# Attention over image pixels: steps of two key tiles for 256 queries, and sums in two of four banks

## The reference

```python
xf = x.reshape(b, c, n)                                   # 8, 128, 1024
q = einsum('oc,bcn->bon', Wq, xf) + bq[None, :, None]     # 64 x 1024
k = einsum('oc,bcn->bon', Wk, xf) + bk[None, :, None]
v = einsum('oc,bcn->bon', Wv, xf) + bv[None, :, None]     # 128 x 1024
attn = softmax(einsum('bci,bcj->bij', q, k), axis=-1)     # 1024 x 1024
out = einsum('bcn,bmn->bcm', v, attn)
return gamma * out + x
```

## Time and profile before

| | |
|---|---|
| median of 3 runs | 234.23 us (234.16 to 234.97) |
| the profiled execution | 234.46 us, its span 232.6 us |
| granted clock of PE in it | 0.996 of full speed |
| PE busy | 221.2 us, 95% |
| DVE, ACT, POOL busy | 175.9, 179.3, 200.4 us (76%, 77%, 86%) |
| DMA moved | 24.39 MB, mean 105 GB/s |

### The profile page before, as it was taken

How to read it: one execution, slowest core, us unless ns; L and a number is a source line. 1 busy time by engine, 2 the same in 40 slices (tenths; PEclk the granted TensorE clock), 3 DMA queues, 4 the chain that set the end, 5 groups by cost and what they waited for, 6 DMA issues and landing times.

```text
span 232.6 us, 4731 instructions
## 1 busy us (share of the span) xinstructions
PE 221.2 (95%) x1608; PEld 189.2 (81%) x1608; DVE 175.9 (76%) x289; ACT 179.3 (77%) x345; POOL 200.4 (86%) x174
## 2 busy tenths in 40 slices
PE   6997999999999999999999999999999999999981
PEld 5464988888788878889789988898798899899880
DVE  1687388796888877796978968797878969696374
ACT  2768887788688877789787886789777878788942
POOL 8688998589996899789996899968996998879990
PEclk9999999999999999999999999999999999999998
DMA  3637900670709325490527607192215803011002
GB/s 85 204 151 175 272 7 2 138 184 3 224 14 232 75 70 159 99 219 3 168 60 175 143 0 230 34 231 55 98 41 120 195 4 135 2 48 45 0 3 90
DMA packets 18023, 24.39 MB, mean 105 GB/s; under 512 B 9936, under 2 KB 10832, under 8 KB 18000
## 3 DMA queue, kind: packets, MB, share of 16 engines
q1 hardware_dynamic: 17552, 23.89, 39.6%
q10 hardware_dynamic: 448, 0.20, 0.3%
HBM read 8.59 MB, written 4.19 MB: 55 GB/s over the span
## 4 chain that ended last, share of the span: by engine, by line
POOL 56%; issue 24%; PE 11%; DVE 4%; ACT 1%; DMA 1%; POOLq 1%; ACTq 0%
POOL weight_lo L458 38%; POOL x_turned_sb L466 7%; POOL total L472 6%; POOL values_b L450 3%; POOL x_lo L439 3%; DVE neg_max L822 2%; PE sums L597 2%; PE work L541 2%; DMA w_qk<-in_L_conv_Wk 1%; PE scores L578 1%; PE scores L579 1%; PE scores L535 1%; PE sums L613 1%; PE scores L639 1%; PE sums L524 1%
## 5 line engine op out<-in xcount | busy, mean ns | idle before, releaser
L458 POOL TENSOR_TENSOR weight_lo<-weight,weight_hi 128x512 bf16<-128x512 f32 x90 | 122.9, 1387 | 21.0 <-ACT weight_hi L756 20.9
L822 DVE TENSOR_REDUCE neg_max<-work 128x1 f32<-128x512 f32 x120 | 80.8, 684 | 26.5 <-PE work L541 26.4
L753 ACT ACTIVATE weight<-scores 128x512 f32<-128x512 f32 x128 | 76.9, 601 | 19.4 <-PE scores L579 14.2
L597 PEld LDWEIGHTS sums<-values,weight_hi 128*128 128x128 f32 x504 | 77.2, 188 | 10.6 <-issue 0.5
L597 PE MATMUL sums<-values,weight_hi 128*128 128x258 f32 x504 | 80.6, 282 | 0.1
L756 ACT ACTIVATE weight_hi<-scores 128x512 fp32r<-128x512 f32 x128 | 77.0, 601 | 0.0
L578 PE MATMUL scores<-q_hihi,k_hilo 128*128 128x512 f32 x128 | 53.4, 417 | 0.7 <-ACT weight_hi L756 0.7
L541 PE MATMUL work<-k_hilo,q_hihi 128*128 128x512 f32 x120 | 48.6, 409 | 2.0 <-DVE neg_max L822 1.6
L579 PE MATMUL scores<-q_lomax,k_hione 128*128 128x512 f32 x128 | 50.4, 394 | 0.0
L853 DVE TENSOR_TENSOR weight_lo<-weight,weight_hi 128x512 bf16<-128x512 f32 x38 | 39.1, 1028 | 4.5 <-ACT weight_hi L756 4.5
L613 PE MATMUL sums<-values_b,weight_lo 128*128 128x130 bf16 x496 | 34.3, 221 | 0.0
(11 more groups left out here) (80 smaller groups left out, 162.3 us busy)
## 6 DMA issues: line engine op xcount, KB each, us to landing
x_turned_sb<-in_x_turned SPq DMA_DIRECT2D x8, 512.0 KB, 5.3
out<-y_sb SPq DMA_DIRECT2D x15, 256.0 KB, 2.5
x_sb<-in_x SPq DMA_DIRECT2D x7, 512.0 KB, 4.7
q_hihi<-qk_hi SPq DMA_DIRECT2D x12, 256.0 KB, 4.2
q_lomax<-qk_lo SPq DMA_DIRECT2D x7, 256.0 KB, 5.0
k_hione<-qk_hi SPq DMA_DIRECT2D x7, 256.0 KB, 5.0
k_hilo<-qk_hi SPq DMA_DIRECT2D x6, 256.0 KB, 3.1
k_hilo<-qk_lo SPq DMA_DIRECT2D x6, 256.0 KB, 5.0
```

The costliest lines, as they stand in the source:

```text
L458: pool.tensor_tensor(weight_lo[:, r], weight[:, r], weight_hi[:, r], ALU.subtract).then_inc(weight_lo_pool_done, 1)
L597: last = pe.matmul(sums[:, it, 0:VCOLS], weight_hi[:, r, tile(it)], values[p][:, j], start=(j == 0), stop=False)
L753: act.activation(weight[:, r], scores[:, s % 2], ACT.Exp)
L822: dve.reduce_max(neg_max[:, t, h:h + 1], place, AX.X, negate=True).then_inc(neg_max_done, 1)
```

## The change

- A step has two key tiles and 256 queries. Its scores are four matmuls of 256 columns, its sums four matmuls of 258 columns: two key tiles by two query tiles. ACT's instructions keep their size.
- A part is four steps: 256 queries against all 1024 keys. Its two query tiles take two of the four banks of `sums`, and the next part takes the other two. A low burst ends each part.
- At a part's end ACT copies the first half of the sums of both tiles, DVE inverts two denominators and adds the copy to the sums in place, in PSUM, and one loop later it makes y of each tile from PSUM with one instruction (multiply by the inverse, add `x_turned_sb`). `total` and POOL's `scale` are gone.
- PE waits for y of the part before last ahead of a part's first sums, in place of `sums_freed`.
- The second v projection moves from step 1 of its own image to step 13 of the image before, POOL's bias additions from steps 7 and 14 to steps 11 and 15 of the image before, x's remainders from 4 and 6 to 3 and 7; `DVE_LOW` loses one of five steps.
- The last part has two tiles; DVE does all of it: inverse, first half times inverse plus x, second half times inverse plus that. Its stores are one on SP and one on ACT.
- In the ramp the first scores need the maxima of two query tiles only; the other two follow as a second rounding, transposition (`mt` at step 0) and row. q of image 0's second half, the second v projection and image 1's q/k projections come behind the first scores, the remainder of that v is DVE's. `load_x_turned(0)` is issued ahead of `spread_by_halves`. The early maxima are shared out anew.

```diff
+PAIR = 2
+PART = PAIR * TILE
+PARTS = CHUNKS * CHUNK_TILES // PAIR
+PART_STEPS = ALL_STEPS // PARTS
...
-DVE_LOW = (0, 4, 8, 13, 15)
+DVE_LOW = (0, 4, 8, 12)
...
-EARLY_MAXES = {5: (2, 0, 1), 6: (2, 1, 2), 7: (2, 3, 2), 8: (2, 5, 1), 9: (2, 6, 1), 10: (2, 7, 1),
-               11: (3, 0, 2), 12: (3, 2, 1), 13: (3, 3, 1), 14: (3, 4, 1), 15: (3, 5, 1), 16: (3, 6, 1), 17: (3, 7, 1)}
+EARLY_MAXES = {0: (1, 1, 2), 1: (1, 3, 2), 2: (1, 5, 2), 3: (1, 7, 1),
+               6: (2, 0, 1), 7: (2, 1, 2), 8: (2, 3, 1), 9: (2, 4, 1), 10: (2, 5, 1), 11: (2, 6, 2),
+               12: (3, 0, 1), 13: (3, 1, 1), 14: (3, 2, 1), 15: (3, 3, 2), 16: (3, 5, 1), 17: (3, 6, 2)}
...
-    if k == 1 and b > 0:
-        jobs.append(("v", b, 1))
+    if b == 0 and k == 0:
+        jobs.append(("mt", 0, 1))
     if b == 0 and k == 4:
         jobs.append(("mt", 1, 0))
     if k in (8, 12) and b + 2 < BATCHES:
         jobs.append(("qk", b + 2, (8, 12).index(k)))
-    if k == 9 and b + 1 < BATCHES:
-        jobs.append(("v", b + 1, 0))
+    if k in (9, 13) and b + 1 < BATCHES:
+        jobs.append(("v", b + 1, (9, 13).index(k)))
...
+FIRST_ORDER = [(0, 0), (1, 0), (0, 1), (1, 1), (2, 0), (3, 0), (2, 1), (3, 1)]
+
+
+def first_bank(t, h):
+
+    return t if t < PAIR and h == 0 else t - PAIR if h == 0 else PAIR + t % PAIR
+
+
+def finish_step(part):
+    return PART_STEPS * part + PART_STEPS + AHEAD + (2 if part == 0 else 0)
...
                 load_x(n)
+            load_x_turned(0)
             spread_by_halves()
-            for n in range(2):
-                load_x_turned(n)
+            load_x_turned(1)
...
-                if k == 3 and b > 0:
-                    scale(2 * b - 1)
-                if k == 11:
-                    scale(2 * b)
-                if k in (7, 14):
-                    add_bias(2 * b + (7, 14).index(k))
-                if k == 2 and b > 0:
-                    short_values(b, 1)
-                if k in (4, 6) and b + 2 < BATCHES:
-                    rest_of_x(b + 2, (4, 6).index(k))
-                if k == 10 and b + 1 < BATCHES:
-                    short_values(b + 1, 0)
+                if s == 0:
+                    short_values(0, 1)
+                if s == 1:
+                    first_q_lo(1)
+                if s in (4, 6):
+                    add_bias((4, 6).index(s))
+                if k in (11, 15) and b + 1 < BATCHES:
+                    add_bias(2 * (b + 1) + (11, 15).index(k))
+                if k in (3, 7) and b + 2 < BATCHES:
+                    rest_of_x(b + 2, (3, 7).index(k))
+                if k in (10, 14) and b + 1 < BATCHES:
+                    short_values(b + 1, (10, 14).index(k))
...
-                h, j, p = k // TILES, k % TILES, b % 2
-                if j == 0:
-                    wait_max_row(pe, HALVES * b + h)
+                h, half, p = k // TILES, k % TILES // PART_STEPS, b % 2
+                if s % PART_STEPS == 0:
+                    wait_max_row(pe, HALVES * b + h, half)
+                if s == TILES:
+                    pe.wait_ge(first_q_lo_done, HALVES)
                 if k == 0 and b > 0:
                     pe.wait_ge(spread_rest[p], loads(b, SPREAD_REST))
                 wait(pe, weight_hi_done, s - 1)
-                pe.matmul(scores[:, s % 2], k_hilo[p][:, tile(j)], q_hihi[p][:, chunk(h)], start=True, stop=False)
-                pe.matmul(scores[:, s % 2], k_hione[p][:, tile(j)], q_lomax[p][:, chunk(h)],
-                          start=False, stop=True).then_inc(scores_done, 1)
+                at = h * CHUNK + half * PART
+                queries = slice(at, at + PART)
+                for kt in range(PAIR):
+                    keys = tile(key_tile(s, kt))
+                    place = scores[:, s % 2, kt * PART:(kt + 1) * PART]
+                    pe.matmul(place, k_hilo[p][:, keys], q_hihi[p][:, queries], start=True, stop=False)
+                    last = pe.matmul(place, k_hione[p][:, keys], q_lomax[p][:, queries], start=False, stop=True)
+                last.then_inc(scores_done, 1)
...
+                if j == 0:
+
+                    wait(pe, y_done, PAIR * (u - 1))
                 pe.wait_ge(weight_hi_done, s + 1)
-                for it in range(CHUNK_TILES):
-                    if j == 0 and it % HALF_TILES == 0:
-
-                        wait(pe, sums_freed, 2 * (c - 1) + it // HALF_TILES + 1)
-                    last = pe.matmul(sums[:, it, 0:VCOLS], weight_hi[:, r, tile(it)], values[p][:, j],
-                                     start=(j == 0), stop=False)
+                for kt in range(PAIR):
+                    for it in range(PAIR):
+                        last = pe.matmul(sums[:, u % 2 * PAIR + it, 0:VCOLS], weight_hi[:, r, part_tile(kt, it)],
+                                         values[p][:, key_tile(s, kt)], start=(j == 0 and kt == 0), stop=False)
...
+                for it in range(PAIR):
+                    for i in steps:
+                        for kt in range(PAIR):
+                            last = pe.matmul(sums[:, u % 2 * PAIR + it, CHANNELS:VCOLS], weight_lo[:, i % RING, part_tile(kt, it)],
+                                             values_b[p][:, key_tile(i, kt)], start=False, stop=(i == s and kt == 1))
+                last.then_inc(sums_done, 1)
...
+            first_max(0)
+            first_max(1)
...
+            pe.wait_ge(first_lo_done, HALVES)
+            first_max(2)
+            first_max(3)
+            pe.wait_ge(w_v_ready, 1)
+            project_v(0, 0, scores[:, 0])
+            first_max(4)
+            first_max(5)
+            first_max(6)
+            pe.wait_ge(neg_max_r_done, 1)
+            pe.wait_ge(pool_setup, SETUP_MADE)
+            turn_max(0, range(PAIR), scores[:, 1])
+            first_max(7)
             project_first(FIRST[3])
-            pe.wait_ge(first_lo_done, HALVES)
-            pe.wait_ge(w_v_ready, 1)
-            for half in range(HALVES):
-                project_v(0, half, scores[:, half])
-                for t in tiles_of_half(half):
-                    pe.wait_ge(neg_max_done, t + 1)
-                    max_scores(0, t, 1, sums[:, t])
+            pe.wait_ge(first_q_lo_done, 1)
+            pe.wait_ge(first_ones_done, HALVES * 16)
+            pe.wait_ge(first_v_done, 1)
+            for s in range(AHEAD):
+                score_tile(s)
+
+            pe.wait_ge(neg_max_done, CHUNK_TILES + 1)
+            project_v(0, 1, sums[:, 0])
             pe.wait_ge(first_hi_done, len(FIRST))
             for name, c, i in FIRST_MAXES:
                 do_max(c, i)
-            pe.wait_ge(neg_max_done, CHUNK_TILES + 1)
-            project_qk(1, 0, sums[:, 0])
-            pe.wait_ge(neg_max_r_done, 1)
-            pe.wait_ge(pool_setup, SETUP_MADE)
-            turn_max(0, sums[:, 2])
-            project_qk(1, 1, sums[:, 1])
...
+            for h in range(HALVES):
+                pe.wait_ge(neg_max_done, CHUNK_TILES + PAIR + h + 1)
+                project_qk(1, h, sums[:, PAIR + h])
...
+                        pe.wait_ge(first_v_rest_done, 1)
+                        pe.wait_ge(neg_max_done, CHUNK_TILES + PAIR)
+                    if s == LAG + PART_STEPS:
+
                         pe.wait_ge(qk_lo_done, HALVES)
-                        pe.wait_ge(max_rows_done, 1)
...
+            for it in range(PAIR):
+                place = sums[:, u % 2 * PAIR + it]
+                for i in range(ALL_STEPS - LAG, ALL_STEPS):
+                    for kt in range(PAIR):
+                        pe.matmul(place[:, 0:VCOLS], weight_hi[:, i % RING, part_tile(kt, it)],
+                                  values[p][:, key_tile(i, kt)], start=False, stop=False)
+                for i in range(ALL_STEPS - PART_STEPS, ALL_STEPS):
                     if it == 0:
                         wait_low(pe, i)
-                    last = pe.matmul(sums[:, it, CHANNELS:VCOLS], weight_lo[:, i % RING, tile(it)], values_b[p][:, i % TILES],
-                                     start=False, stop=(i == ALL_STEPS - 1))
+                    for kt in range(PAIR):
+                        last = pe.matmul(place[:, CHANNELS:VCOLS], weight_lo[:, i % RING, part_tile(kt, it)],
+                                         values_b[p][:, key_tile(i, kt)], start=False, stop=(i == ALL_STEPS - 1 and kt == 1))
                 last.then_inc(sums_done, 1)
...
+            def take_low_sum(u):
+                act.wait_ge(sums_done, u + 1)
+
+                wait(act, total_done, u - 1)
+                act.activation(low_sum[:, u % 2], sums[:, part_banks(u), 0:CHANNELS], ACT.Copy).then_inc(low_sum_done, 1)
...
-            write_max_rows(0, sums[:, 2])
-            round_qk(1, 0, sums[:, 0])
-            for s in range(AHEAD):
-                exponentials(s)
-            round_qk(1, 1, sums[:, 1])
+            write_max_rows(1, 0, 0, PART, scores[:, 1])
+            first_q(1, bank(0))
+            exponentials(0)
+            round_v(0, 1, sums[:, 0])
+            exponentials(1)
```

(58 more changed lines are left out.)

## The result

After the change the kernel takes 242.59 us (median of four runs, 242.46 to 242.75); the kernel before took 234.54 us in the runs beside it (234.16 to 234.97). The ratio is 1.034, with a 95% interval of 1.032 to 1.036. Each ratio in this document compares with executions of the kernel before that ran beside the kernel in question; a few slow ones, at a lower clock, are left out. The prediction said 228.8 us and had the sign wrong. The profiled execution has a span of 241.0 us where the one before has 232.6, so 8.4 us are to be found.

A forecast was written before the change was run, and what follows sets the result against it. PE was taken as the bound, plus 0.87 us per image lost to a DVE lump. +1.0 (split matmuls) - 2.8 (steady images) - 3.3 (banks and tail) - 0.3 (ramp) = -5.4 us, giving 228.8 us; range 225.3 to 233.6.

The forecast's parts named there:

- What bounds the kernel, and the place of the stall: PE's own columns bound it, plus 0.87 us per image of PE standing in loops 8 and 9 behind a DVE lump.
- Split score matmuls, +1.0: Four score matmuls of 256 columns per step instead of two of 512: +1.0 us over 128 steps, between 0 and 2.0.
- Rival D: Weight loads of the small score matmuls aren't covered: 25.6 us more, 254 us; chance 0.04.
- Parts of two banks and the tail, -3.3: Last image's bank wait goes (-0.45 us) and the end after the last exponential shortens from 9.2 to 6.4 us: -3.3 together.
- DVE's new instructions: y instructions of 128 columns at 0.34 us beside a busy POOL, in-place PSUM additions at 0.42 us.
- Rival E: DVE becomes the bound, with additions at 0.85 us and y at 0.41: 243.3 us; chance 0.08.
- The low weights on DVE: In DVE's sum per image, one low weights instruction removed at 1.03 us; total from 22.0 to 21.6 us.
- Steady images, -2.8: Stall at steps 8/9 falls from 0.87 to about 0.1 us, 0.3 left per image: -2.8 us, bounds -4.3 and 0.
- rival B: The stall stays or moves, to steps 12/13 or ACT's waits for low sums: 231.6 us; chance 0.18.
- 12/13: Steps 12/13 of each image get 0.15 to 0.5 us of stall from the moved v remainder on DVE.
- Rival C: PE was held by banks only in the last image, ramp gives back 1.0, half the tail: 233.6 us; chance 0.10.
- The ramp, -0.3: First score some 2.6 us earlier, near 13.7, but moved work leaves step 5 only 0.3 us earlier; bounds +1.5 and -2.3.

The follow-up runs named there:

- Experiment 4: The kernel before, with each score matmul of 512 columns made as two of 256 with a weight load each: 235.42 us, ratio 1.002.
- experiment 7: experiment 3 with the second v projection put back from step 13 to step 1 of its own image: 235.60 us, ratio 1.002.
- experiment 5: experiment 3 with the low weights of step 12 of each image on POOL too: 231.19 us, ratio 0.983.
- experiment 6: experiment 3 with DVE making the low weights of step 13 instead of step 12: 231.32 us, ratio 0.985.
- experiment 11: experiment 9, but in image 0 DVE makes the low weights of steps 8 and 13: 229.46 us, ratio 0.976.
- experiment 3: The kernel after, with image 0's second bias on POOL moved from step 6 to 8, second remainder of x from 7 to 9: 234.77 us, ratio 1.000.
- experiment 8: The kernel after, with only image 0's second remainder of x on POOL moved from step 7 to 9: 242.84 us, ratio 1.033.
- experiment 2: The kernel after, with DVE making step 8's low weights by a one-operand reduction, leaving out the subtraction: 238.72 us, ratio 1.017.
- experiment 1: The kernel after, with the low weights of step 8 on POOL, DVE's first being step 12's: 241.19 us, ratio 1.027.
- experiment 9: experiment 3 with DVE making the low weights of steps 0, 4, 9 and 13: 236.69 us, ratio 1.007.
- experiment 10: experiment 9 with image 0's early maxima spread from step 5 on: 235.28 us, ratio 1.002.

## Why the prediction was wrong, point by point

**What bounds the kernel, and the place of the stall: right.** PE is the bound, and a lump on DVE stood in its way at steps 8/9: taking the lump away shortened that stall from 0.87 to 0.25 us.

**Split score matmuls, +1.0: right.** In the starts of PE's timeline after, a step's four sums take 0.47 us (66.56 to 67.03) and its four scores of 256 columns 0.48 us (67.03 to 67.51), 0.12 us each as forecast:

```profile
66.56 0.64 PE L612 MATMUL sums<-values,weight_hi 128*128 128x258 f32 x4
67.03 0.28 PE L592 MATMUL scores<-q_hihi,k_hilo 128*128 128x256 f32 x1
...
67.51 0.39 PE L548 MATMUL work<-k_hilo,q_hihi 128*128 128x512 f32 x1
```

Experiment 4 gives 7 ns a step, 0.9 us in all. Rival D is out.

**Parts of two banks and the tail, -3.3: right.** Measured is -3.17 from step 112 to the end, the v projection taken out. The bank wait in the last image is gone: two score starts right behind a low burst were 1.47 us apart and are 1.04 apart now (229.83 and 230.87). From the last step's score to the end the kernel after takes 8.2 us and the one before 11.0, 2.8 less. The tail's working can be followed in the rows of all engines after:

```profile
232.73 3.78 POOL L472 TENSOR_TENSOR weight_lo<-weight,weight_hi 128x512 bf16<-128x512 f32 x3 [1.06 <-ACT weight_hi L781]
233.98 0.63 ACT L781 ACTIVATE weight_hi<-scores 128x512 fp32r<-128x512 f32 x1
237.23 0.64 PE L725 MATMUL sums<-values_b,weight_lo 128*128 128x130 bf16 x8
238.50 0.35 DVE L986 SCALAR_TENSOR_TENSOR y_sb<-sums,one_over,with_x 128x128 f32<-128x128 f32 x1
```

POOL ends at 236.51, 1.9 us after the last exponential, and the span ends 6.4 us after it. Both numbers are those of the prediction; before it was 9.2 us.

**DVE's new instructions: right.** y takes 343 ns in the mean of 62 and never over 353, also beside a busy POOL; the addition in place 413 ns (forecast 0.34 and 0.42). Rival E's prices for them (0.41 and 0.85 us) are refuted. Its total of 243.3 us lies near the measured 242.59 by luck: the period of the steady images is 27.3 us and not 28.8, and the loss is in image 0, of which E says nothing. These groups are by line and shape (busy us, mean ns):

```profile
L903 DVE SCALAR_TENSOR_TENSOR y_sb<-sums,one_over,x_turned_sb 128x128 f32<-128x128 f32 x62 | 18.7, 343 | 0.7 <-DVE sums L883 0.4
L883 DVE TENSOR_TENSOR sums<-sums,low_sum 128x256 f32<-128x256 f32 x31 | 12.8, 413 | 0.0
L878 DVE TENSOR_TENSOR weight_lo<-weight,weight_hi 128x512 bf16<-128x512 f32 x30 | 47.7, 1590 | 0.0
```

**The low weights on DVE: the term that failed.** The last of these lines is where the sum broke. The prediction took L853's mean of 1.03 us as the price of each low weights instruction on DVE, and applied its own finding (two SBUF operands, POOL in the way) to the y instructions that left and not to the low weights that stayed. Their mean went to 1.59 us, their longest from 1.55 to 6.64. DVE is busy for 22.9 us in image 2 where the prediction has 21.6. A mean of an instruction that contends is not a price; it is a record of what it happened to meet. Without the long one the mean is still 1.42 (47.7 - 6.64 over 29).

**Steady images, -2.8: wrong, +1.44 in images 2 to 5.** This is rival B's mechanism: the stall moved to 12/13. B had it at 231.6 us. (Rival C's sum of 233.6 leaves out the 1.0 us that its own sentence has the ramp give back; with it C is at 234.6, which changes nothing here.) The forecast left 0.3 us per image for it, for a v remainder that has nothing to do with it (experiment 7). It was 0.9 in all, of the low weights of step 12 (experiments 5, 6), and 0.25 was left at 8/9. With both placed one step later, the image takes 26.2 us: 0.7 less than before in each of images 2 to 5 (2.95 us in all), 0.3 below the 26.5 forecast.

**The ramp, -0.3: wrong by 8.4 us (it is +8.07), the step that decides the sign.** The first score was right (13.71, forecast 13.7), but step 5 came at 23.22 against 23.25 us where 0.3 early was forecast; the timeline has two new waits of PE before it, 0.36 (ACT's first q) and 0.56 us. At step 11 it was 0.46 us ahead of before. Then came the interval of 11.06 us. The prediction followed DVE's and PE's queues through the ramp and never laid POOL's beside them: it costed the moved biases at "nothing", since POOL's sum stays below PE's and the load that they wait for comes early enough, and the moved remainder of x has no term in it at all. Nobody did wait for their results. DVE waited for POOL to stop. Its bound of +1.5 us for the ramp had no room for that.

Image 1 hides another 1.5 us, which comes from the redone ramp and is in every kernel of this study with it, experiment 11 too (27.75 us against 26.2). Intervals 17/18 and 19/20 are 1.78 and 3.10 us where image 2 has 1.21 and 2.10. At 19/20 a second maxima matmul stands in one step, and PE waits 0.49 us for DVE at 57.12. That the maxima left over from the ramp cause this is read from the rows and was not tried by itself.

**Why experiment 11 comes out at the forecast.** Against before it has +0.86 to step 16, +0.79 in image 1, -2.95 in images 2 to 5, +0.15 in image 6 and -4.15 behind step 112, in all -5.3 us. With the v projection's 0.87 us counted back, the ramp is 0.0 (forecast -0.3), the last image and the tail -3.3 (forecast -3.3), and images 1 to 6 are -2.0 (forecast +1.0 for the split matmuls, most of it here, and -2.8 for the stall). In images 2 to 5 the gain is larger than forecast and image 1 gives 1.5 us of it back.

**What stays open.** Experiments 3 and 8 show that POOL's bias at that place makes the loss, and experiment 2 that an instruction with one SBUF operand is not held. What decides whether DVE gets in between two POOL instructions the runs do not tell. Where the next one of POOL's still waited for its exponential, DVE always got in (experiments 3, 11). Where POOL had no gap, DVE was passed over up to four times in a row in image 0 (the kernel after, experiments 1, 8, 9 and 10), but got in behind the first POOL instruction at step 12 of experiment 3 and in the steady images. How early the input of POOL's next instruction was ready does not sort the cases: 1.4 us early DVE got in (experiment 3, 39.55), 0.2 us early it did not (experiment 2, 40.71, the exponential ended at 40.50). Nor was it tried whether any gap put into POOL's row would do, or how the two waits early in the ramp could be avoided.

## What to carry to other kernels

When side work is moved on POOL, lay its new queue beside DVE's and look where a DVE instruction with two SBUF operands falls beside POOL instructions that are all ready: its price there can be the length of POOL's whole row, and PE pays it if a maximum stands behind it in DVE's queue. Such instructions belong behind what PE waits for, and where POOL waits for someone (here: low weights waiting for ACT) they took 0.68 us. And take the spread of an instruction's duration, not its mean, as a sign that it shares something; then look for its longest case in the new order before costing a move at nothing.

## What the runs showed of the hardware

- A DVE subtraction of 128x512 with both operands in SBUF took from 0.68 us (POOL idle or waiting) to 6.64 us (five POOL instructions without a gap); 6.63, 5.89, 5.64, 5.27 and 2.83 us in other kernels. Between two POOL instructions of the steady images that leave no gap it took up to 1.74 us, and POOL's second then took 1.7 in place of 1.3. A reduction reading one such operand took 0.68 us beside the same row as the one of 6.64, y from PSUM and SBUF 0.335 to 0.353 us in the kernel after, and the addition in place in PSUM 0.411 to 0.414 us.
- PE's clock was granted at 0.51, the 1.2 GHz level, in 38.0 to 43.5; it had fallen while PE stood for 5.57 us, and was 1.00 from 43.5 on. That made a stall of 5.6 us cost some 8. In experiment 2 PE waited 1.92 us and the clock was 0.51 from 44.5 to 48.0. With stalls of 0.9 us in each image it stayed at 1.00.
- A float32 score matmul of 256 columns with its weight load starts 0.12 us after the last, in a stream of them; splitting 512 into two of 256 cost 0.65 us in the 96 steps of images 1 to 6, 7 ns a step.
